# A two-layer gated attention kernel: K projection at steps 7 to 10, output projection at steps 13 to 16, and another order on GpSimd

## The chip, the cores and the metric

The kernel runs on one core of one Trainium2 chip. The metric is the device time of one execution in microseconds (us). A core has five engines with queues of their own, which meet only through semaphores: TensorE (PE, matmuls; its weight loads are shown as PEld), VectorE (DVE), ScalarE (ACT), GpSimd (POOL) and SyncE (SP, which here only issues DMAs).

## The reference, cut to what matters

x has 32 batches of 256 rows and 256 columns, each with a context of 120 rows and 512 columns. Four sublayers are added to x one after the other, each with a gate tanh(g):

```python
def xattn0(x, context, w_qkv, w_proj, b_proj):          # 16 heads of 16
    q, k, v = heads(x @ w_qkv.T)
    k = concat(heads_k(context), k); v = concat(heads_v(context), v)   # 120 + 256 keys
    attn = softmax(q * D ** -0.5 @ k.T)
    return (attn @ v) @ w_proj.T + b_proj
x = x + tanh(g_xattn[0]) * xattn0(layernorm(x), ctx, ...)
x = x + tanh(g_ffn[0])   * ternary_ffn(layernorm(x), ...)   # scale: max |x| over all batches
x = x + tanh(g_xattn[1]) * depool(layernorm(x), ctx, lens)  # recurrence over 120 patches
x = x + tanh(g_ffn[1])   * int8_ffn(layernorm(x), ...)
```

The second sublayer divides by one maximum over all batches. So the kernel has two phases: first the attention sublayer for all 32 batches, then a row phase with the other three. The change is in the first phase.

## The kernel before

**Loop and steps.** In the attention phase every engine runs the same loop over batches, `iterations`, each with its own `body` (a few batches are written out ahead of and behind a hardware loop over pairs). A body of batch b has 24 steps, u = 0 to 23. The engines don't share a clock for the steps; each works its list in order and waits on semaphores. A batch has 16 heads, 256 queries (two tiles of 128) and 376 keys in 3 tiles of 128.

**What TensorE does in a step.** `scores_t(u)`, line 592: two matmuls of transposed scores into one of three banks st_ps, of which ScalarE takes the exponential into probs (line 883, one for each step, at the end of the step on its list). Because of the three banks, the scores of step u wait for the exponential of step u - 3. `scores`, line 602: the same scores in the other layout (ms_ps, two banks), for batch b's last heads and the next batch's first 12 heads, of which VectorE takes the row maximum (line 787); one or two in a step, 32 in a batch. `attend`, line 617: 12 groups of matmuls of probs with V at steps 1, 7, 13 and 19, into pv_ps, which ScalarE copies out as oT (line 899).

**The jobs.** Between these stand the small products and transposes of the `JOBS` table. Two banks are shared, `misc` (0) and `aux` (1). An entry (bank, first step, steps, batch offset) says where a job's matmuls go; a job of four steps has one piece, two matmuls, in each. On misc: xT (transposes of the normalised rows), q, k and v (projections, lines 640 and 643) and proj (output projection, line 648). On aux: o0 to o3 (transposes of oT, line 664), aT (of the attention rows, line 669), neg0 and neg1 (of the split maxima, line 658) and kcT (of the context's keys, line 653). A job's first piece waits until the engine that reads the bank has taken the job before it (`s_free`), and the reader waits for `s_full`. ScalarE takes xT (line 904), q (918), k (951), kcT (945), v (962), aT (921) and the negs (891, followed by a DMA into q6, line 893); VectorE takes o0 to o3 (`normalise`, a reciprocal at line 794 and a multiplication at 796) and proj (line 829, which updates x).

**How Q and K come to the scores.** GpSimd splits qk, which holds Q, K and the context's keys of batch b + 2, into three bf16 parts: four instructions (lines 531 to 537) for each half m of the heads. SyncE's `stack` copies them with 12 DMAs for each half into q6 and k6, which the scores of step 6 (first half) and step 18 (second half) of the next body read. The maxima take a like way: GpSimd's `split_neg` (lines 468 to 474), neg0 or neg1 on TensorE, a copy and a DMA by ScalarE, and then the scores of step 0 or 12.

**GpSimd's order in a body:** maxima of the second half (b), the context's norm (485 to 493), the norm of x for b + 3 (498 to 504), a wait for ScalarE's normalised rows and the bias (507), distances (511), row statistics of b - 1 (515 to 518), maxima of the first half (b + 1), and both halves of the split (b + 2).

## Time and profile before

| | us |
|---|---|
| median of 3 runs (lowest to highest) | 1210.75 (1209.83 to 1213.24) |
| profiled execution | 1212.96 |
| its span, first to last instruction | 1211.2 |
| TensorE busy in it | 1078.1 (89%) |
| VectorE | 921.0 (76%) |
| ScalarE | 818.8 (68%) |
| GpSimd | 700.3 (58%) |

The granted TensorE clock was 1.00 through the attention phase, 0.97 over the span. The attention phase fills about four fifths of the span, the row phase the rest. Busy shares are means; TensorE's ends are modelled, so starts are the surer numbers. In a time line a row is a start, a duration, engine, line, operation, output and inputs, how many instructions were merged, and in brackets the idle time before it with what ended it. A row of several merged instructions has the duration of all together.

### The profile page before, as it was taken

Reading aid. Unit: us, or ns where it says so; the run is one execution under the profiler, and the core shown is the slowest. Engines: PE = TensorE matmul, PEld = TensorE weight load, DVE = VectorE, ACT = ScalarE, POOL = GpSimd, SP = SyncE. Lnnn points to the kernel's source line nnn. Section 1 sums busy time; section 2 is a strip of 40 time slices with the busy share of each in tenths; the row PEclk is TensorE's granted clock in tenths of the full one; section 3 lists DMA queues with packets and bytes.
Section 4 is the critical chain, followed back from the end, with each engine's and each line's share of the span. In section 5 each row is a group of like instructions: output and inputs, shape, how many; then the busy total and the mean of one; then the engine's idle time right before and its main releaser. Section 6 shows DMA issues by size and latency. Waiting matters only on the chain.

```text
span 1211.2 us, 33412 instructions
## 1 busy us (share of the span) xinstructions
PE 1078.1 (89%) x8458; PEld 706.5 (58%) x8458; DVE 921.0 (76%) x2328; ACT 818.8 (68%) x1730; POOL 700.3 (58%) x1259
## 2 busy tenths in 40 slices
PE   4599899989999999999999999999999886988885
PEld 3355555656565665555566555656655445877774
DVE  3877777767777777777777777777777646999997
ACT  2157666766777777677677777777766566888874
POOL 4355555555555555555555555555554416777776
PEclk9699999999999999999999999999999997999997
DMA  4233333333333333333333333333333300222232
GB/s 125 78 92 96 96 96 94 94 94 94 98 100 100 100 99 99 103 101 99 100 99 100 97 104 101 97 94 95 87 87 87 83 12 31 68 84 93 85 92 86
DMA packets 158681, 110.18 MB, mean 91 GB/s; under 512 B 17155, under 2 KB 154789, under 8 KB 158629
## 3 DMA queue, kind: packets, MB, share of 16 engines
q1 hardware_dynamic: 156900, 108.78, 33.1%
q10 hardware_dynamic: 1728, 0.79, 0.2%
q8 instruction: 23, 0.38, 0.1%
q14 instruction: 30, 0.24, 0.1%
HBM read 30.30 MB, written 16.29 MB: 38 GB/s over the span
## 4 chain that ended last, share of the span: by engine, by line
PE 33%; DVE 17%; issue 15%; POOL 15%; DMA 9%; SPq 5%; POOLq 2%; DVEq 2%; ACT 1%; ACTq 0%
PE pv_ps L617 8%; PE ms_ps L602 6%; PE st_ps L592 6%; DMA q<-parts 6%; POOL qk L533 4%; PE misc L648 4%; DVE neg L787 4%; PE misc L640 3%; SPq L394 3%; POOL parts L531 2%; POOL parts L535 2%; SPq L392 2%; POOL parts L537 2%; DMA q<-negT 2%; DVE am L1171 2%
## 5 line engine op out<-in xcount | busy, mean ns | idle before, releaser
L787 DVE TENSOR_REDUCE neg<-ms_ps 128x1 f32<-128x376 f32 x1024 | 533.0, 545 | 221.2 <-PE ms_ps L602 212.7
L883 ACT ACTIVATE probs<-st_ps 128x512 f32<-128x512 f32 x768 | 440.2, 603 | 103.2 <-PE st_ps L592 102.6
L602 PE MATMUL ms_ps<-k,q 96*128 96x376 bf16 x1024 | 334.7, 328 | 33.8 <-DMA q<-parts 25.2
L592 PE MATMUL st_ps<-q,k 99*128 99x256 bf16 x1536 | 295.3, 274 | 10.2 <-DMA q<-negT 6.9
L592 PEld LDWEIGHTS st_ps<-q,k 99*128 99x128 bf16 x1536 | 131.8, 98 | 140.3 <-issue 43.3
L617 PE MATMUL pv_ps<-probs,v 128*32 128x256 f32 (+1 forms) x3072 | 195.4, 387 | 0.1
L602 PEld LDWEIGHTS ms_ps<-k,q 96*128 96x128 bf16 x1024 | 98.8, 97 | 104.5 <-DVE neg L787 66.7
L640 PE MATMUL misc<-xnT,wqkvT 128*128 128x256 f32 x512 | 158.1, 394 | 1.5 <-ACT xnT L904 1.5
L507 POOL TENSOR_TENSOR xs<-xs,bias_p 128x256 f32 (+1 forms) x64 | 45.2, 727 | 161.0 <-ACT xn L941 161.0
L617 PEld LDWEIGHTS pv_ps<-probs,v 128*32 128x32 f32 (+1 forms) x3072 | 87.5, 110 | 81.2 <-issue 24.3
L640 PEld LDWEIGHTS misc<-xnT,wqkvT 128*128 128x128 f32 x512 | 95.0, 200 | 5.9 <-ACT xnT L904 2.3
L899 ACT COPY oT<-pv_ps 128x256 f32<-128x256 f32 x128 | 47.2, 369 | 74.2 <-PE pv_ps L617 74.1
L537 POOL TENSOR_TENSOR parts<-qk,parts 128x632 bf16<-128x632 f32 x64 | 88.8, 1387 | 13.1 <-POOL parts L535 13.1
L533 POOL TENSOR_TENSOR qk<-qk,parts 128x632 f32<-128x632 f32 x64 | 88.7, 1385 | 11.7 <-POOL parts L531 11.7
L643 PE MATMUL misc<-wqkvT,xnT 128*128 128x256 f32 x256 | 77.0, 382 | 0.3 <-ACT qk L951 0.3
L648 PE MATMUL misc<-wprojT,attnT 128*128 128x256 f32 x256 | 75.8, 379 | 0.8 <-ACT attnT L921 0.8
L1099 PE MATMUL st_ps<-winT,probs 128*128 128x256 f32 x256 | 66.6, 382 | 0.7 <-ACT probs L1219 0.7
L1067 PE MATMUL ms_ps<-ident,probs 128*128 128x128 f32 x256 | 44.0, 300 | 22.1 <-DVE probs L1196 14.2
L511 POOL TENSOR_SCALAR plug<-plug,iota_n 120x256 f32<-120x256 f32 x32 | 37.0, 1155 | 36.0 <-DMA plug<-plugs 36.0
L891 ACT COPY negT<-aux 24x256 bf16<-24x256 bf16 x64 | 23.2, 362 | 48.7 <-PE aux L658 48.7
L531 POOL TENSOR_SCALAR parts<-qk 128x632 bf16<-128x632 f32 x64 | 46.1, 720 | 15.5 <-issue 13.4
L535 POOL TENSOR_SCALAR parts<-qk 128x632 bf16<-128x632 f32 x64 | 46.3, 723 | 12.5 <-POOL qk L533 12.5
(185 smaller groups left out, 1751.6 us busy)
## 6 DMA issues: line engine op xcount, KB each, us to landing
k<-parts SPq DMA_DIRECT2D x384, 94.0 KB, 2.8
q<-parts SPq DMA_DIRECT2D x384, 64.0 KB, 2.5
xs<-in_x SPq DMA_DIRECT2D x32, 256.0 KB, 2.8
out_dram<-xn SPq DMA_DIRECT2D x32, 256.0 KB, 2.2
cx<-in_ctx SPq DMA_DIRECT2D x32, 240.0 KB, 3.3
recurrence_input<-u_in SPq DMA_DIRECT2D x32, 120.0 KB, 2.3
plug<-plugs SPq DMA_DIRECT2D x32, 120.0 KB, 3.5
powers<-gath SPq DMA_DIRECT2D x32, 120.0 KB, 3.3
```

Source lines behind the costliest of these rows:

```text
L531: pool.tensor_scalar(parts[:, m, 0, :], f, 1.0, 0.0, ALU.mult, ALU.add).then_inc(s_split, 1)
L533: pool.tensor_tensor(f, f, parts[:, m, 0, :], ALU.subtract).then_inc(s_split, 1)
L535: pool.tensor_scalar(parts[:, m, 1, :], f, 1.0, 0.0, ALU.mult, ALU.add).then_inc(s_split, 1)
L537: pool.tensor_tensor(parts[:, m, 2, :], f, parts[:, m, 1, :], ALU.subtract).then_inc(s_split, 1)
L592: mm = pe.matmul(st_ps[u % SR][:, j * S:(j + 1) * S], k6[0:KM, r, h, k * P:(k + 1) * P], q6[0:KM, r, h, :], start=True, stop=True)
L602: pe.matmul(ms_ps[t][:, 0:KEYS], q6[0:KR, r, h % HU, t * P:(t + 1) * P], k6[0:KR, r, h % HU, 0:KEYS], start=True, stop=True).then_inc(s_ms, 1)
L617: mm = pe.matmul(pv_ps[VW * j:VW * (j + 1), 0:S], v[0:rows, pB, k, HG * g + j, :], probs[0:rows, (2 * w + j // 2) % PR, j % 2 * S:(j % 2 + ...
L640: mm = pe.matmul(misc[:, x0 * S:(x0 + 1) * S], wqkvT[:, x1, at:at + P], xnT[:, par, x1, :], start=(x1 == 0), stop=(x1 == KT - 1), skip_gro ...
L643: mm = pe.matmul(misc[:, x0 * C:(x0 + 1) * C], xnT[:, opp, x1, x0 * P:(x0 + 1) * P], wqkvT[:, x1, 2 * C:3 * C], start=(x1 == 0), stop=(x1 ...
L648: mm = pe.matmul(misc[:, x0 * C:(x0 + 1) * C], attnT[:, x1, x0 * P:(x0 + 1) * P], wprojT[:, x1, :], start=(x1 == 0), stop=(x1 == KT - 1), ...
L787: dve.tensor_reduce(neg[:, m, t, h % HU:h % HU + 1], ms_ps[t][:, 0:KEYS], AX.X, ALU.max, negate=True).then_inc(s_red, 1)
L883: act.activation(probs[:, u % PR, :], st_ps[u % SR][:, :], ACT.Exp).then_inc(s_exp, 1)
```

## The change

The K projection moves from steps 14 to 17 to steps 7 to 10, the output projection from 8 to 11 to 13 to 16, and the context keys' transposes from step 12 to step 2. ScalarE's copies follow: K at step 11 instead of 18, the context's preparation at 0 instead of 10, the context keys at 3 instead of 15, the attention rows at 7 instead of 6; its two normalised halves stand at 10 and 12 instead of both at 13; the powers' exponential moves from 11 to 15. VectorE updates x at step 17 instead of 13, takes the statistics at 19 and 21 instead of 15 and 18, the row maxima and minima of x at 7 and 13 (both a batch later) instead of 19 and 7, and the powers' update at 23 instead of 20. On GpSimd the first half of the split comes ahead of the bias, then the maxima, the distances, the second half, and the row statistics last. SyncE stacks the first half ahead of the powers' store. What is computed stays the same.

```diff
         JOBS = {
-            "xT": (0, 0, 1, 2), "q": (0, 2, 4, 2), "proj": (0, 8, 4, -1), "k": (0, 14, 4, 2), "v": (0, 19, 4, 1),
-            "o3": (1, 4, 1, -1), "aT": (1, 6, 1, -1), "neg1": (1, 8, 1, 0), "o0": (1, 10, 1, 0),
-            "kcT": (1, 12, 1, 2), "o1": (1, 16, 1, 0), "neg0": (1, 20, 1, 1), "o2": (1, 22, 1, 0),
+            "xT": (0, 0, 1, 2), "q": (0, 2, 4, 2), "k": (0, 7, 4, 2), "proj": (0, 13, 4, -1), "v": (0, 19, 4, 1),
+            "kcT": (1, 2, 1, 2), "o3": (1, 4, 1, -1), "aT": (1, 6, 1, -1), "neg1": (1, 8, 1, 0), "o0": (1, 10, 1, 0),
+            "o1": (1, 16, 1, 0), "neg0": (1, 20, 1, 1), "o2": (1, 22, 1, 0),
         }
...
+                if live(b + 2):
+                    stack(b + 2, par, 0)
                 if live(b - 1):
                     own_wait(sp, s_decay, b)
                     sp.dma_start(powers_dram[b - 1], gath[0:NP, opp, :]).then_inc(d_pow[opp], 16)
-                if live(b + 2):
-                    stack(b + 2, par, 0)
...
                     pool.tensor_tensor(rn0[:, 2, :], rn0[:, 1, :], mv0[:, :, 0], ALU.mult).then_inc(s_rn0, 1)
+                if live(b + 2):
+                    split(b, 0, i, par, opp)
+                if live(b + 3):
+                    B = b + 3
                     pool.wait_ge(s_xn, B * 2 + 2)
                     for t in range(T):
                         pool.tensor_tensor(xs[:, B, t, :], xs[:, B, t, :], bias_p[:, :], ALU.add).then_inc(s_xb, 1)
+                if live(b + 1):
+                    split_neg(b + 1, 0, b)
                 if live(b):
 
                     own_wait(pool, d_plug[par], i * 16 + 16)
                     pool.tensor_scalar(plug[0:NP, par, :], plug[0:NP, par, :], 0.0, iota_n[0:NP, :], ALU.add, ALU.add).then_inc(s_dist, 1)
+                if live(b + 2):
+                    split(b, 1, i, par, opp)
...
-                if live(b + 1):
-                    split_neg(b + 1, 0, b)
-                if live(b + 2):
-                    for m in range(2):
-
...
-                    if u == 13 and live(b - 1):
+                    if u == 17 and live(b - 1):
...
-                    if u == 15 and live(b - 1):
+                    if u == 19 and live(b - 1):
...
-                    if u == 18 and live(b - 1):
+                    if u == 21 and live(b - 1):
...
-                    if u == 19 and live(b - 1):
+                    if u == 7 and live(b - 2):
+                        dve.tensor_reduce(mx1[:, bass.ds((b - 2) * T, T)], xs[:, b - 2, :, :], AX.X, ALU.max).then_inc(s_x1, 1)
+                    if u == 13 and live(b - 2):
+                        dve.tensor_reduce(mn1[:, bass.ds((b - 2) * T, T)], xs[:, b - 2, :, :], AX.X, ALU.min).then_inc(s_x1, 1)
+                    if isinstance(b, int) and b == LAST and u == 22:
                         dve.tensor_reduce(mx1[:, bass.ds((b - 1) * T, T)], xs[:, b - 1, :, :], AX.X, ALU.max).then_inc(s_x1, 1)
-                    if u == 7 and live(b - 2):
-                        dve.tensor_reduce(mn1[:, bass.ds((b - 2) * T, T)], xs[:, b - 2, :, :], AX.X, ALU.min).then_inc(s_x1, 1)
-                    if isinstance(b, int) and b == LAST and u == 21:
                         dve.tensor_reduce(mn1[:, bass.ds((b - 1) * T, T)], xs[:, b - 1, :, :], AX.X, ALU.min).then_inc(s_x1, 1)
-                    if u == 20 and live(b):
+                    if u == 23 and live(b):
...
                 for u in range(HS):
+                    if u == 0 and live(b + 2):
+                        act.wait_ge(d_cx[par], (i + 1) * 16 + 16)
+                        if live(b + 1):
+                            wait_full(act, b - 1, "kcT")
+                        for m in range(2):
...
+                        ins.then_inc(s_cxp, 1)
...
+                    if u == 3 and live(b + 2):
+                        wait_full(act, b, "kcT")
+                        if live(b + 1):
+                            act.wait_ge(s_split, (b + 2) * 8)
+                        act.copy(qk[:, :, 2 * S:FC], aux[:, 0:2 * P].rearrange("p (m r) -> p m r", m=2)[:, :, 0:NP]).then_inc(s_free[1], 1)
...
-                        if live(b + 1):
-                            act.wait_ge(s_split, (b + 2) * 8)
                         act.mul(qk[:, :, 0:S], misc[:, :].rearrange("p (m r) -> p m r", m=2), SCALE).then_inc(s_free[0], 1)
-                    if u == 6 and live(b - 1):
+                    if u == 7 and live(b - 1):
...
-                    if u == 10 and live(b + 2):
...
-                    if u == 13 and live(b + 3):
+                    if u == 10 and live(b + 3):
...
-                        for t in range(T):
-                            act.activation(xn[:, opp, t, :], xs[:, B, t, :], ACT.Identity, bias=rn0[:, 3, t:t + 1],
-                                           scale=rn0[:, 1, t:t + 1]).then_inc(s_xn, 1)
-                    if u == 15 and live(b + 2):
-                        wait_full(act, b, "kcT")
-                        act.copy(qk[:, :, 2 * S:FC], aux[:, 0:2 * P].rearrange("p (m r) -> p m r", m=2)[:, :, 0:NP]).then_inc(s_free[1], 1)
-                    if u == 11 and live(b - 1):
+                    if u in (10, 12) and live(b + 3):
+                        t = (u - 10) // 2
+                        act.activation(xn[:, opp, t, :], xs[:, b + 3, t, :], ACT.Identity, bias=rn0[:, 3, t:t + 1],
+                                       scale=rn0[:, 1, t:t + 1]).then_inc(s_xn, 1)
+                    if u == 11 and live(b + 2):
+                        wait_full(act, b, "k")
+                        act.copy(qk[:, :, S:2 * S], misc[:, :].rearrange("p (m r) -> p m r", m=2)).then_inc(s_free[0], 1)
+                    if u == 15 and live(b - 1):
                         act.wait_ge(s_plug, b)
                         act.activation(gath[0:NP, opp, :], gath[0:NP, opp, :], ACT.Exp, scale=-DT).then_inc(s_decay, 1)
-                    if u == 18 and live(b + 2):
-                        wait_full(act, b, "k")
-                        act.copy(qk[:, :, S:2 * S], misc[:, :].rearrange("p (m r) -> p m r", m=2)).then_inc(s_free[0], 1)
...
-                    if u == 19 and live(b + 1):
+                    if u == 17 and live(b + 1):
...
+                    if u == 21 and live(b + 1):
+                        neg_rows(b + 1, opp, 0, live(b))
```

GpSimd's new function `split(b, m, ...)` holds the same waits and the same four instructions as the loop that is taken out, for one half m.

Three places in the order, in the body of batch 1, which stands written out ahead of the hardware loop. First TensorE from step 11 to the first output of step 14; before, with the last piece of the output projection (line 648) in step 11, the context transposes (653) in step 12, the attention product (617) in step 13 and the K projection (640) in step 14:

```order
L592 MATMUL st_ps<-q,k 128x256 x2
L602 MATMUL ms_ps<-k,q 128x376
L648 MATMUL misc<-wprojT,attnT 128x256
L592 MATMUL st_ps<-q,k 128x256 x2
L602 MATMUL ms_ps<-k,q 128x376
L653 MATMUL aux<-ident,cxp 128x120 x2
L592 MATMUL st_ps<-q,k 128x256 x2
L602 MATMUL ms_ps<-k,q 128x376
L617 MATMUL pv_ps<-probs,v 32x256 x12
L592 MATMUL st_ps<-q,k 128x256 x2
L602 MATMUL ms_ps<-k,q 128x376
L640 MATMUL misc<-xnT,wqkvT 128x256
```

After, where the scores are lines 597 and 607 and the output projection is line 653:

```order
L597 MATMUL st_ps<-q,k 128x256 x2
L607 MATMUL ms_ps<-k,q 128x376
L597 MATMUL st_ps<-q,k 128x256 x2
L607 MATMUL ms_ps<-k,q 128x376
L597 MATMUL st_ps<-q,k 128x256 x2
L607 MATMUL ms_ps<-k,q 128x376
L653 MATMUL misc<-wprojT,attnT 128x256
L622 MATMUL pv_ps<-probs,v 32x256 x12
L597 MATMUL st_ps<-q,k 128x256 x2
L607 MATMUL ms_ps<-k,q 128x376
L653 MATMUL misc<-wprojT,attnT 128x256
```

Steps 11 and 12 hold nothing but scores now, and a piece of the output projection stands in front of the attention product of step 13.

ScalarE from the copy of the maxima (step 8) to the exponentials of steps 11 and 12; before:

```order
L891 COPY negT<-aux 24x256
L893 DMA q<-negT 3x8x256
L883 ACTIVATE probs<-st_ps 128x512 x2
L929 COPY cxp<-cx 120x128 x2
L883 ACTIVATE probs<-st_ps 128x512
L948 ACTIVATE gath<-gath 120x256
L883 ACTIVATE probs<-st_ps 128x512 x2
L936 ACTIVATE rn<-rn 128x2
L941 ACTIVATE xn<-xs,rn 128x256 x2
L883 ACTIVATE probs<-st_ps 128x512
```

After, where 889 is the exponential, 945 and 951 the normalisation, 955 the copy of K:

```order
L897 COPY negT<-aux 24x256
L899 DMA q<-negT 3x8x256
L889 ACTIVATE probs<-st_ps 128x512 x2
L945 ACTIVATE rn<-rn 128x2
L951 ACTIVATE xn<-xs,rn 128x256
L889 ACTIVATE probs<-st_ps 128x512
L955 COPY qk<-misc 128x2x256
L889 ACTIVATE probs<-st_ps 128x512
L951 ACTIVATE xn<-xs,rn 128x256
L889 ACTIVATE probs<-st_ps 128x512 x2
```

The first normalised half now stands ahead of the exponential of step 10, in the place of the context copy, and the copy of K follows that exponential.

VectorE from the row maxima of steps 13 to 15 to those of step 19; before, with the update of x (829) at step 13 and its statistics (834) at step 15:

```order
L787 TENSOR_REDUCE neg<-ms_ps 128x1 x4
L829 SCALAR_TENSOR_TENSOR xs<-misc,tg,xs 128x512
L787 TENSOR_REDUCE neg<-ms_ps 128x1 x3
L834 BN_STATS bn<-xs 128x6 x2
L787 TENSOR_REDUCE neg<-ms_ps 128x1
L794 RECIPROCAL rcp<-aux 128x8
L796 TENSOR_TENSOR attn<-aux,rcp 128x2x64
L787 TENSOR_REDUCE neg<-ms_ps 128x1 x3
L840 BN_AGGR mvt<-bn 128x2 x2
```

After, where 792 are the maxima, 834 the update of x, 839 its statistics:

```order
L799 RECIPROCAL rcp<-aux 128x8
L801 TENSOR_TENSOR attn<-aux,rcp 128x2x64
L792 TENSOR_REDUCE neg<-ms_ps 128x1 x2
L834 SCALAR_TENSOR_TENSOR xs<-misc,tg,xs 128x512
L792 TENSOR_REDUCE neg<-ms_ps 128x1 x2
L839 BN_STATS bn<-xs 128x6 x2
L792 TENSOR_REDUCE neg<-ms_ps 128x1 x3
```

Between the normalisation of step 16 and the V projection of step 19 there is now the update of x, with two maxima ahead of it.

## Rows read from the trace of the kernel before

**Rows 1.** Page, part 1: busy time, share of the span and instructions of each engine.

```profile
PE 1078.1 (89%) x8458; PEld 706.5 (58%) x8458; DVE 921.0 (76%) x2328; ACT 818.8 (68%) x1730; POOL 700.3 (58%) x1259
```

**Rows 2.** Chain that ended last, 400 to 560 us: start us, us, what.

```profile
445.79 0.73 POOL parts L531
...
456.36 0.33 PE ms_ps L602
...
485.27 0.33 PE ms_ps L602
```

**Rows 3.** Time line of TensorE, steps 6 and 8: columns as told above.

```profile
456.36 0.33 PE L602 MATMUL ms_ps<-k,q 96*128 96x376 bf16 x1 [0.75 <-DMA q<-parts]
456.58 0.63 PE L669 MATMUL aux<-ident,attn 128*128 128x128 f32 x4
...
459.88 0.28 PE L658 MATMUL aux<-identb,negp 128*24 128x128 bf16 x2
```

**Rows 4.** Time line of VectorE, step 5, the normalisation.

```profile
455.54 0.20 DVE L794 RECIPROCAL rcp<-aux 128x8 f32<-128x8 f32 x1
455.77 0.29 DVE L796 TENSOR_TENSOR attn<-aux,rcp 128x128 f32<-128x128 f32 x1
```

**Rows 5.** Time line of ScalarE, steps 8 to 18.

```profile
461.60 1.09 ACT L883 ACTIVATE probs<-st_ps 128x512 f32<-128x512 f32 x2 [1.04 <-PE st_ps L592]
462.57 0.71 ACT L929 COPY cxp<-cx 120x128 f32<-120x128 f32 x2
463.18 0.61 ACT L883 ACTIVATE probs<-st_ps 128x512 f32<-128x512 f32 x1
...
464.93 0.23 ACT L936 ACTIVATE rn<-rn 128x2 f32<-128x2 f32 x1
465.29 1.09 ACT L941 ACTIVATE xn<-xs,rn 128x256 f32 x2
...
469.92 0.59 ACT L951 COPY qk<-misc 128x512 f32<-128x512 f32 x1
```

**Rows 6.** Time line of TensorE, steps 12 to 20.

```profile
463.55 0.40 PE L653 MATMUL aux<-ident,cxp 120*128 120x120 f32 x2
463.84 0.39 PE L592 MATMUL st_ps<-q,k 99*128 99x256 bf16 x2
...
464.33 1.50 PE L617 MATMUL pv_ps<-probs,v 128*32 128x256 f32 x24
465.76 0.39 PE L592 MATMUL st_ps<-q,k 99*128 99x256 bf16 x2
...
468.38 0.38 PE L664 MATMUL aux<-ident,oT 128*128 128x128 f32 x2
...
470.64 0.62 PE L643 MATMUL misc<-wqkvT,xnT 128*128 128x256 f32 x2
...
472.63 0.39 PE L592 MATMUL st_ps<-q,k 99*128 99x256 bf16 x2
...
474.24 0.28 PE L658 MATMUL aux<-identb,negp 128*24 128x128 bf16 x2 [0.62 <-POOL negp L474]
```

**Rows 7.** Time line of VectorE, steps 13 to 18.

```profile
464.90 0.74 DVE L829 SCALAR_TENSOR_TENSOR xs<-misc,tg,xs 128x512 f32 x1
...
469.21 0.29 DVE L796 TENSOR_TENSOR attn<-aux,rcp 128x128 f32<-128x128 f32 x1
469.42 1.52 DVE L787 TENSOR_REDUCE neg<-ms_ps 128x1 f32<-128x376 f32 x3
```

**Rows 8.** Time line of GpSimd, the split's second half (first half: rows 2).

```profile
450.53 0.72 POOL L531 TENSOR_SCALAR parts<-qk 128x632 bf16<-128x632 f32 x1
```

**Rows 9.** Line 852: ns min/median/max, first and last start; then the first batch's time line.

```profile
L852 DVE SCALAR_TENSOR_TENSOR gath<-plug x32: 415/415/1181, 92.5 to 987.9; 120x256 f32<-120x256 f32 x32
...
92.07 1.38 POOL L533 TENSOR_TENSOR qk<-qk,parts 128x632 f32<-128x632 f32 x1 [0.18 <-POOL parts L531]
92.55 1.18 DVE L852 SCALAR_TENSOR_TENSOR gath<-plug 120x256 f32<-120x256 f32 x1
```

40 lines of the change are left out of this document (17 added, 23 removed).

## The prediction, made before the changed kernel ran

> **What bounds the kernel now.** I read the page's first part, then the chain of work that ended last, then the time lines of TensorE, ScalarE, VectorE and GpSimd for one batch, and compare starts with starts. TensorE is busy 89% of the span, VectorE 76% and ScalarE 68% [rows 1]. The profiled execution took 1212.96 us, the median of the runs is 1210.75; I add to the median. In the chain the same matmul returns after 485.27 - 456.36 = 28.91 us [rows 2]: that is one batch, and what lengthens or shortens it counts for each batch. The chain closes through GpSimd: the split of Q and K begins at 445.79, and the score matmul that reads its result starts at 456.36.
>
> At two places of the batch TensorE visibly waits for that late GpSimd work. At step 6 the scores of the next batch start at 456.36 with 0.75 us of idle time before them, put down to the DMA of the parts [rows 3]. At step 20 the transposes of the maxima start at 474.24 after 0.62 us of waiting for GpSimd [rows 6]. There are smaller holes, and they are what the change leans on: the scores of step 13 start at 463.84, and the exponential of step 10 began at 463.18 and took 0.61, so it ended at 463.79 [rows 5, 6]. There are three score banks, so step 13 must wait for step 10's exponential: here ScalarE sets the pace, not TensorE.
>
> I place the new work in this one batch, on the clock of before, from step 6 to step 6.
>
> **Step 6 and 7: a gain that is spent at once.** Now the K copy comes at step 11 instead of 18, and the split of the first half stands right behind the norm on GpSimd. It can start near 464.8. From the start of a split to the score matmul it took 456.36 - 445.79 = 10.57 us [rows 2]; so it is done near 475.4, and step 6 of the next batch is at 484. The wait at step 6 goes. What is late next is the transposes of the attention rows behind it: they wait for VectorE's normalisation, which starts its multiplication at 455.77 and takes 0.29, so they start at 456.12 instead of 456.58 [rows 3, 4], a gain of 0.46. But a piece of the K projection now stands in step 7. What a piece in front of the attention product costs: step 19's piece starts at 470.64 and step 20 at 472.63, 1.99 us, and the product alone takes 465.76 - 464.33 = 1.43 [rows 6], so 0.56. That is 0.1 more than the gain; the product had a small hole in front of it in step 7 that this piece fills. I take the net as zero: the transposes of the maxima at step 8 stay at 459.88 [rows 3].
>
> **Steps 8 to 14: +0.79 us.** ScalarE copies the maxima, issues their DMA and starts exponentials 8 and 9 at 461.60 as before [rows 5]. At 462.57 it had the context copy (0.71) and then exponential 10. Now it has at step 10 the small multiplication and one normalised half: 465.29 - 464.93 = 0.36 and half of 1.09 less overlap, 0.50 [rows 5]. Exponential 10 starts at 462.57 + 0.86 = 463.43, 0.25 later than before, and ends at 464.04. Scores of step 13 start at 464.09. Behind it on ScalarE stands the K copy: it starts 0.49 after exponential 10 (two take 1.09, one 0.60 [rows 5]), at 463.92, takes 0.59 [rows 5], ends at 464.51. The output projection's first piece is in step 13, and needs the bank that this copy frees: 464.57. With the 0.56 and the product's 1.43, step 14 starts at 466.56, against 465.76 before: **+0.79** (rounding the sum). What the change takes out of steps 11 and 12 (a projection piece, and the two context transposes with 463.84 - 463.55 = 0.29 [rows 6]) gives nothing back, as TensorE waits for exponential 10 anyway. The bounds of this term: 0.25 if only exponential 10 moved, 0.8 as worked out, and 1.0 if the DMA of the maxima is also late for step 12.
>
> **Steps 14 to 20: +0.38 us.** From step 14 to the transposes at step 16 it was 468.38 - 465.76 = 2.62 us [rows 6], with the same pieces in it, so these start at 469.17. The V projection at step 19 takes the bank that VectorE's update of x frees, and the update has moved from step 13, where 3 steps lay behind it, to step 17. VectorE must first do the normalisation (it needs the transposes, which last 0.38 [rows 6], so 469.17 + 0.42), one row maximum, a second, and then the update: 469.59 + 0.23 to the multiplication [455.77 - 455.54, rows 4], + 0.21 to the next maximum [469.42 - 469.21, rows 7], two maxima at a third of 1.52 each, and 0.74 for the update [rows 7]: 471.8. The V projection started at 470.64 [rows 6]; now at 471.81, **+1.17** in all, so +0.38 on top of 0.79. Queued on TensorE behind this waiting piece are the attention product of step 19 and all that follows. Low bound 0: VectorE could be earlier, as the statistics (step 15) left the stretch.
>
> **Step 20: -0.62 us.** With the maxima's split on GpSimd in front of the second half and of the row statistics, does TensorE still wait? Without a wait TensorE would come there 1.17 later and 0.62 earlier, at 474.24 + 1.17 - 0.62 = 474.79. On GpSimd the first half starts near 464.8 and takes 450.53 - 445.79 = 4.74 us [rows 2, 8], to 469.5. Two bias additions and four small instructions lie between that and 474.79, and the last maximum that the four need ends on VectorE at about 471.1 (469.59 + 0.23 + 0.21 + 0.5 + 0.55). That leaves 3.7 us for four instructions on 16 columns. The wait of 0.62 [rows 6] goes whole: +1.17 - 0.62 = +0.55. What it would cost if GpSimd were late after all: up to that 0.62 again.
>
> **Step 2: +0.29 us.** The context transposes now stand in step 2, where TensorE has no hole, at 0.29 us [rows 6]. The context copy on ScalarE at step 0 (0.71) has cover: its next reader, the first Q piece at step 2, is 2 us on, behind the attention product.
>
> **Sum.** 0.79 + 0.38 - 0.62 + 0.29 = 0.84 us a batch; each start is read to about 0.05, and I round down to 0.8. Batches with all of it are 28 of 32: the first has no output projection, the last three lack the normalisation or K. 28 x 0.8 = 22.4, and 1210.75 + 22.4 = **1233 us**. Prologue, tail and the row phase after the attention keep their work: 0, within 2 us. The extra moves cost nothing where cover is long: SyncE's powers store behind the first half's 12 DMAs, the second half of the split (its reader is step 18 of the next batch), the two reductions over x at steps 7 and 13 instead of 19 and 7.
>
> [...] VectorE's update of the recurrence powers reads the same SBUF tile twice. Its median is 0.415 us and its longest 1.181 [rows 9]: at 92.55 it began while GpSimd's subtraction of the split (92.07, 1.38 long) ran, and took 1.18. The change moves it to step 23, beside the second half's split, at nearly each batch. On VectorE this is 0.77 us more, and the next maxima are late by that. TensorE then needs them at step 2, behind the 1.43 us product of step 1, so I count 0. [...]
>
> **Rivals.**
> Rival 1, faster: both new waits are covered. TensorE is late for step 13 by no more than now, because ScalarE reaches exponential 10 earlier once TensorE no longer stalls at step 6, and the update of x finds VectorE empty since the statistics have left steps 15 to 18. For it: VectorE is busy only 76% [rows 1]. Against: starts at 463.79 and 463.84 fit too well for slack. Then only -0.62 + 0.29 remains, -0.33 a batch, and with the 0.1 or so that step 7 may keep, -0.4: 28 x 0.4 = 11, **1199.5 us**. It decides if the K copy ends before TensorE is at step 13.
> Rival 2, no change: the first term is 0.25 (the K copy is covered) and the second 0: 0.25 - 0.62 + 0.29 = -0.08, about **1209 us**.
> Rival 3, slower still: the 0.77 us of the blocked update is not covered at step 1. 28 x 0.77 = 21.6 more, 1255 us; with half of it covered **1244 us**. Against: the product of step 1 lies between.
> The change does what it says: steps and queue order are fixed in the program.
>
> **Chances.** Forecast (1224 to 1242 us): 0.62. Rival 1: 0.20. Rival 2: 0.10. Rival 3: 0.08. A measurement of this kernel tells a change from none at about 0.3%, 3.6 us. Slower by more: 0.62 + 0.08 = 0.70; within: 0.10; faster: 0.20. The range of 8 in 10 reaches to 1200, which takes in Rival 2 and the slower half of Rival 1, and to 1244 for Rival 3: 1200 to 1244.
>
> **What the profile of the changed kernel would show.** The chain's period would be 29.7 us instead of 28.91. No idle time for the DMA of the parts before the scores of step 6, and none for GpSimd before the transposes of step 20. The scores of step 13 would start about 4.2 us after the transposes of step 8 (now 463.84 - 459.88 = 3.96), and the output projection's first piece within 0.1 us of the K copy's end. The V projection would start within 0.1 us of the end of VectorE's update of x. The update of the powers would take about 1 us in most batches. I am wrong if the output projection's first piece follows its scores with no hole, or if the V projection waits for its maxima alone; and if ScalarE stands at step 0 for the context load, a further term is missing.

## The result and the profile after

The changed kernel took 1234.54 us, the median of 4 runs (1233.35 to 1236.48), beside 1211.99 us for the kernel before (4 runs, 1209.83 to 1214.72). The ratio is 1.0186 with a 95% interval of 1.0159 to 1.0213: slower. The prediction was 1233 us.

Part 1 of the page of the changed kernel, which answers to rows 1, and the shares of its chain by engine:

```profile
PE 1083.7 (88%) x8458; PEld 711.5 (58%) x8458; DVE 923.6 (75%) x2328; ACT 826.0 (67%) x1730; POOL 703.8 (57%) x1259
...
PE 54%; DVE 18%; issue 11%; ACT 5%; POOL 4%; DMA 4%; DVEq 1%; ACTq 1%; POOLq 0%; SPq 0%
```

The engines do the same work as before in a longer span. GpSimd has 4% of the chain that ended last, where it had 15% in the kernel before. The loop through its split, which the prediction followed in rows 2, is open: TensorE no longer waits for the parts. The other engines' waits now make up the period. The chain of the changed kernel in the same stretch, 400 to 560 us (start, us, what):

```profile
464.65 0.63 PE aux L674 x4
...
473.34 0.73 POOL parts L485
...
478.08 0.72 POOL xs L528
479.49 0.75 DVE xs L834
...
494.34 0.63 PE aux L674 x4
```

The GpSimd rows in it are no wait. The chain takes the last event of a semaphore for the releaser, and the update of x (L834) does wait for the semaphore of the bias additions (L528); but by the program it needs only the additions of its own batch, which were made three bodies earlier, and VectorE had no idle time before 479.49.

The period is 494.34 - 464.65 = 29.69 us. In the kernel before it was 28.91 from one score matmul to the next [rows 2], and 28.95 from these transposes (456.58) to the next ones (485.53). TensorE's time line of one batch of the changed kernel, steps 6 to 20 (columns as in rows 3: start, us, engine, line, what, and in brackets the idle time before it and what ended it). L674 are the attention rows' transposes, L663 those of the maxima (steps 8 and 20), L597 the scores, L653 the output projection, L648 the V projection:

```profile
464.65 0.63 PE L674 MATMUL aux<-ident,attn 128*128 128x128 f32 x4 [0.43 <-DVE attn L801]
...
468.38 0.28 PE L663 MATMUL aux<-identb,negp 128*24 128x128 bf16 x2
...
472.29 0.39 PE L597 MATMUL st_ps<-q,k 99*128 99x256 bf16 x2 [0.97 <-DMA q<-negT]
...
472.68 0.38 PE L597 MATMUL st_ps<-q,k 99*128 99x256 bf16 x2
472.90 0.32 PE L607 MATMUL ms_ps<-k,q 96*128 96x376 bf16 x1
473.06 0.65 PE L653 MATMUL misc<-wprojT,attnT 128*128 128x256 f32 x2
473.65 1.50 PE L622 MATMUL pv_ps<-probs,v 128*32 128x256 f32 x24
475.09 0.39 PE L597 MATMUL st_ps<-q,k 99*128 99x256 bf16 x2
...
480.28 0.70 PE L648 MATMUL misc<-wqkvT,xnT 128*128 128x256 f32 x2 [0.32 <-DVE xs L834]
...
483.27 0.28 PE L663 MATMUL aux<-identb,negp 128*24 128x128 bf16 x2
```

From these starts and those of rows 3 and 6 the batch can be cut at the same five places in both kernels. The last column is the mean difference over the batches whose attention transposes start between 270 and 870 us (21 before, 20 after). All numbers in us:

| stretch | before | after | difference | the prediction's term | mean difference |
|---|---|---|---|---|---|
| attention transposes, step 6, to maxima transposes, step 8 | 3.30 | 3.73 | +0.43 | +0.46 (gain of step 6 given back) | +0.44 |
| to the scores of step 14 | 5.88 | 6.71 | +0.83 | +0.79 | +0.96 |
| to the V projection, step 19 | 4.88 | 5.19 | +0.31 | +0.38 | +0.31 |
| to the maxima transposes, step 20 | 3.60 | 2.99 | -0.61 | -0.62 | -0.63 |
| to the attention transposes of the next batch | 11.29 | 11.07 | -0.22 | -0.46 + 0.29 | -0.20 |
| period | 28.95 | 29.69 | +0.74 | +0.84 | +0.88 |

The batch shown is one of the shorter ones (they last 29.45 to 30.05). What varies is the second stretch, from 6.54 to 7.06.

The spans of the two profiled executions differ by 1231.6 - 1211.2 = 20.4 us. Of these, 3.3 are there before the first attention transposes (103.6 and 106.9 us). The six batches behind them give back 0.7, since the kernel before had slow batches there (up to 30.81). The next 20 batches cost 17.6, and the rest 0.2.

The waits that the prediction named on other engines are there too. ScalarE, then VectorE, of the same batch:

```profile
469.17 0.75 ACTq L899 DMA_DIRECT2D q<-negT  x1
...
471.92 0.58 ACT L889 ACTIVATE probs<-st_ps 128x512 f32<-128x512 f32 x1
472.39 0.57 ACT L955 COPY qk<-misc 128x512 f32<-128x512 f32 x1
```

```profile
479.49 0.74 DVE L834 SCALAR_TENSOR_TENSOR xs<-misc,tg,xs 128x512 f32 x1
```

The update of x ends at 480.23 and the V projection starts at 480.28, and TensorE waited for it. The copy of K ends at 472.96 and the first piece of the output projection starts at 473.06, but this piece did not wait: it follows the scores before it (472.90) after 0.16 us, as it does in the kernel before. So it is in 16 of the 20 batches; in the other four it comes after 0.24, which is 0.05 behind the end of the copy. That the piece would follow with no hole was one of the prediction's own signs of being wrong.

What held TensorE there was not in the sum. At step 12 (472.29) it waits 0.97 us for the small DMA that brings the negated maxima into q, and that DMA was issued at 469.17, 3.12 us earlier; in the middle batches this wait is 0.46 to 1.39 us. In the kernel before, the scores of step 12 start 2.42 us after the issue in nearly all batches, without a wait. So two things stand behind each other at steps 12 to 14, this DMA and ScalarE's order, and end at nearly the same time. The first experiments take them apart.

### The profile page after: what moved, and what is told of

Same layout as the page of the kernel before. It is cut to its first block, busy times and chain, and to the rows that moved or that the text cites. A ratio compares the mean times of both kernels' runs of the same rounds, so it can differ in the third digit from the quotient of the medians.

```text
span 1231.6 us, 33435 instructions
## 1 busy us (share of the span) xinstructions
PE 1083.7 (88%) x8458; PEld 711.5 (58%) x8458; DVE 923.6 (75%) x2328; ACT 826.0 (67%) x1730; POOL 703.8 (57%) x1259
## 4 chain that ended last, share of the span: by engine, by line
PE 54%; DVE 18%; issue 11%; ACT 5%; POOL 4%; DMA 4%; DVEq 1%; ACTq 1%; POOLq 0%; SPq 0%
PE pv_ps L622 14%; PE st_ps L597 9%; PE ms_ps L607 8%; PE misc L645 7%; PE misc L648 5%; DMA q<-negT 3%; PE misc L653 3%; DVE neg L792 3%; ACT probs L889 2%; DVE xs L834 2%; PE aux L674 2%; DVE am L1178 2%; DVE xs L1167 2%; PE misc L637 1%; PE aux L669 1%
## 5 line engine op out<-in xcount | busy, mean ns | idle before, releaser
L889 ACT ACTIVATE probs<-st_ps 128x512 f32<-128x512 f32 x768 | 445.4, 602 | 100.2 <-PE st_ps L597 99.4
L597 PE MATMUL st_ps<-q,k 99*128 99x256 bf16 x1536 | 294.9, 273 | 35.4 <-ACT probs L889 16.5
L597 PEld LDWEIGHTS st_ps<-q,k 99*128 99x128 bf16 x1536 | 131.6, 98 | 163.5 <-ACT probs L889 63.9
L468 POOL TENSOR_SCALAR negp<-neg 128x16 bf16<-128x16 f32 x64 | 13.1, 205 | 201.9 <-DVE neg L792 201.8
L491 POOL TENSOR_TENSOR parts<-qk,parts 128x632 bf16<-128x632 f32 x64 | 88.8, 1387 | 12.4 <-POOL parts L489 12.4
L648 PE MATMUL misc<-wqkvT,xnT 128*128 128x256 f32 x256 | 81.0, 398 | 9.7 <-DVE xs L834 9.7
L653 PE MATMUL misc<-wprojT,attnT 128*128 128x256 f32 x256 | 77.3, 385 | 0.8 <-ACT attnT L938 0.8
L648 PEld LDWEIGHTS misc<-wqkvT,xnT 128*128 128x128 f32 x256 | 44.6, 194 | 18.7 <-DVE xs L834 16.9
L1106 PEld LDWEIGHTS st_ps<-winT,probs 128*128 128x128 f32 x256 | 46.4, 191 | 7.7 <-ACT probs L1226 2.1
```

What stands on the lines that cost most here:

```text
L491: pool.tensor_tensor(parts[:, m, 2, :], f, parts[:, m, 1, :], ALU.subtract).then_inc(s_split, 1)
L597: mm = pe.matmul(st_ps[u % SR][:, j * S:(j + 1) * S], k6[0:KM, r, h, k * P:(k + 1) * P], q6[0:KM, r, h, :], start=True, stop=True)
L648: mm = pe.matmul(misc[:, x0 * C:(x0 + 1) * C], xnT[:, opp, x1, x0 * P:(x0 + 1) * P], wqkvT[:, x1, 2 * C:3 * C], start=(x1 == 0), stop=(x1 ...
L653: mm = pe.matmul(misc[:, x0 * C:(x0 + 1) * C], attnT[:, x1, x0 * P:(x0 + 1) * P], wprojT[:, x1, :], start=(x1 == 0), stop=(x1 == KT - 1), ...
L889: act.activation(probs[:, u % PR, :], st_ps[u % SR][:, :], ACT.Exp).then_inc(s_exp, 1)
L1106: pe.matmul(m1_ps[q][:, t * C:(t + 1) * C], yxT[:, k, t * P:(t + 1) * P], winT[:, k, :], start=(k == 0), stop=False)
```

## Experiments

Each ratio is that of the kernel to the kernel before, with its 95% interval.

**Steps 12 to 14: two holds.** `e2_xn12` takes ScalarE's first normalised half out from ahead of exponential 10, so that the K copy comes earlier.

```diff
-if u in (10, 12) and live(b + 3):
-    t = (u - 10) // 2
+if u == 12 and live(b + 3):
+    for t in range(T):
```

> The changed kernel with both normalised halves at step 12 on ScalarE, none at step 10, so that exponential 10 and the K copy come 0.5 us (one half) sooner. Theory A (step 13 waits for ScalarE's exponential 10, the projection for the K copy): steps 13 and 14 come 0.3 to 0.5 us sooner, 8 to 14 us less than the changed kernel, 1221 to 1226 us. Rival D (the DMA of the maxima lands 3.0 to 3.5 us after its issue and holds step 12, with step 13 0.4 behind it): no gain, 1232 to 1236 us.

Measured: 1232.93 us, ratio 1.0162 [1.0145, 1.0179], as rival D had it. `e3_sp` leaves ScalarE alone. On SyncE the plug load (the distances' input) goes ahead of the store of the recurrence input, and this store goes behind the first stacks and the powers' store.

```diff
-sp.dma_start(input_dram[b + 1], u_in[0:NP, opp, :]).then_inc(d_dep[opp], 16)
...
 sp.dma_start(plug[0:NP, par, :], plug_dram[b].partition_broadcast(NP)).then_inc(d_plug[par], 16)
...
 stack(b + 2, par, 0)
...
 sp.dma_start(powers_dram[b - 1], gath[0:NP, opp, :]).then_inc(d_pow[opp], 16)
+sp.dma_start(input_dram[b + 1], u_in[0:NP, opp, :]).then_inc(d_dep[opp], 16)
```

> The changed kernel with the SyncE order of the run e4 alone: distances' load ahead, recurrence input's store behind the first half's stack and the powers' store. Rival D expects the step 12 landing at 2.4 us instead of 3.3 behind its issue; since exponential 10 ends 4.16 us behind the transposes of step 8 and the K copy 4.6, the gain is only what the landing adds on top, 0.1 to 0.3 us a batch: 1226 to 1232 us. Theory A expects no change.

Measured: 1233.47 us, 1.0176 [1.0147, 1.0205]: no change, as theory A had it. But the landing did come earlier, as rival D had it. `e4_xn12_sp` has both edits.

> As the one before, and on SyncE the store of the recurrence input stands behind the first half's stack and the powers' store, and the distances' load goes out earlier, so that neither goes out beside the DMA of the maxima for step 12. If the landing at step 12 is late because of these two (rival D), it falls from 3.3 us behind its issue to about 2.4, and together with the earlier exponential 10 steps 13 and 14 come 0.8 us sooner: 1208 to 1214 us. If only ScalarE counts (theory A), this is the same as the one before.

Measured: 1222.47 us, 1.0079 [1.0058, 1.01]. Each edit alone gives next to nothing, both together 12 us, though less than was expected (1208 to 1214). The lines of TensorE at step 12 and 13, first of e2_xn12, then of e3_sp:

```profile
470.28 0.39 PE L597 MATMUL st_ps<-q,k 99*128 99x256 bf16 x2 [0.90 <-DMA q<-negT]
```

```profile
469.89 0.39 PE L597 MATMUL st_ps<-q,k 99*128 99x256 bf16 x2
...
470.99 0.39 PE L597 MATMUL st_ps<-q,k 99*128 99x256 bf16 x2 [0.35 <-ACT probs L889]
471.21 0.33 PE L607 MATMUL ms_ps<-k,q 96*128 96x376 bf16 x1
471.46 0.70 PE L653 MATMUL misc<-wprojT,attnT 128*128 128x256 f32 x2
```

In e2_xn12 the DMA wait is left: its maxima DMA was issued at 467.22, 3.06 us before. In e3_sp step 12 (469.89) comes 2.28 us after the issue (467.61), and now step 13 waits for exponential 10, as the prediction had reckoned it, and the output projection's piece starts 0.05 us behind the end of the K copy (in all 20 middle batches). From the maxima transposes to step 14's scores one batch takes 6.71 us in the changed kernel, 6.58 in e2_xn12 (466.43 to 473.01), 6.71 in e3_sp (466.82 to 473.53), 6.26 in e4_xn12_sp (460.65 to 466.91), and 5.88 before. The means over the middle batches are 6.84, 6.72, 6.73, 6.27 and 5.88. So the prediction's cause, ScalarE's order, is by itself enough for +0.85 (e3_sp), and the late DMA, with the K copy still early enough not to be waited for, for +0.84 (e2_xn12). The changed kernel, which has both, has +0.96. With both gone +0.39 is left: in e4_xn12_sp the K copy (464.21, 0.58 long) still ends only just ahead of the piece (464.84) that takes its bank.

**Steps 17 to 20: the update of x.** `e1_v20` moves the V projection one step later.

```diff
-"v": (0, 19, 4, 1),
+"v": (0, 20, 4, 1),
```

> The changed kernel with the V projection at steps 20 to 23 instead of 19 to 22. Theory: the V projection waits 0.6 us at step 19 for VectorE's update of x, with the attention product queued behind it. One step later it does not wait, and the product of step 19 starts about 1 us sooner; the last piece, in step 23, then makes the transposes of step 0 wait about 0.5 us for the V copy. Net about -0.5 us a batch: 1215 to 1223 us. If the update of x is not what holds step 19, the V piece only moves: no change against the changed kernel, or slower by the wait at step 0.

Measured: 1219.55 us, 1.007 [1.0045, 1.0094], as expected. The V projection's wait for VectorE (0.32 us before 480.28 above) is gone from all batches, and with it 15 us. In the middle batches the stretch from the scores of step 14 to the maxima's transposes of step 20 is 1.01 us shorter (7.16 instead of 8.17), and the one behind it, to the attention transposes, 0.46 longer, near the 1 and 0.5 of the expectation; the period is 0.53 shorter. That is more than the wait of 0.32. The move also puts one V piece behind the transposes of step 20, and how much of the gain comes from that was not taken apart.

`e9_three` joins the three edits.

> The changed kernel with three single changes together: both normalised halves at step 12, SyncE's order of the run e3, the V projection at steps 20 to 23. Alone, the first two together gave -0.0107 of the time of before and the third -0.0116. If the two new waits (step 12 to 13, and step 19) are separate terms of a sum, they add: ratio 0.995 to 0.999 to before, 1206 to 1211 us. If both are faces of one loop, the sum falls short: 1.002 to 1.007.

Measured: 1211.72 us, 0.9983 [0.9965, 1.0002]. The ratio lies in the range of a sum (0.995 to 0.999), and one loop (1.002 or more) is ruled out. With the edits against three holds the moved kernel is as fast as the kernel before. The sum is not quite reached, and the trace shows why: the spans of the profiled executions fell by 14.8 us (e1_v20) and 12.0 (e4_xn12_sp), but by 21.7 together, because the DMA of the maxima is now late at step 0. One batch:

```profile
388.28 0.39 PE L597 MATMUL st_ps<-q,k 99*128 99x256 bf16 x2 [1.05 <-DMA q<-negT]
```

This DMA was issued at 384.64, 3.64 us earlier. Beside it SyncE issued the store of the recurrence input (384.34) and the context load (385.04). In four of 21 batches it was on time, used 2.42 us after its issue without a wait; these batches last 28.75 us, less than the 28.93 of the kernel before, and the others from 28.89 to 29.47.

**Step 2: the context transposes.** `e8_kct12` puts them back at step 12, and ScalarE's copy of their result at step 13.

```diff
-"kcT": (1, 2, 1, 2),
+"kcT": (1, 12, 1, 2),
```

> The changed kernel with the context keys' transposes back at step 12 and ScalarE's copy of them at step 13 (the check that the split before is done then stands at step 6 again); the context copy stays at step 0. Theory: at step 2 the two transposes cost TensorE 0.2 to 0.3 us a batch, at step 12 nothing, as TensorE waits there anyway; 6 to 8 us less than the changed kernel, 1226 to 1229 us. The rival, that the hole at step 12 and 13 is not there to be used (the copy on ScalarE delays what follows), expects no change or up to 6 us more.

Measured: 1255.29 us, 1.0337 [1.0302, 1.0371]: 21 us slower than the changed kernel, outside of both theories. Step 2 did lose its transposes, but at step 12 they cost about the same: they stand behind the scores of step 12, and TensorE's wait is ahead of these. The stretch from step 8 to step 14 is 0.20 us longer in the mean. And step 0 now waits, for the same kind of DMA as step 12. TensorE of e8_kct12 at step 0, then ScalarE's issue, then SyncE's issues around it:

```profile
526.17 0.39 PE L597 MATMUL st_ps<-q,k 99*128 99x256 bf16 x2 [1.44 <-DMA q<-negT]
```

```profile
522.58 0.75 ACTq L899 DMA_DIRECT2D q<-negT  x1
```

```profile
522.12 0.37 SPq L416 DMA_DIRECT2D powers<-gath  x1
522.84 0.35 SPq L420 DMA_DIRECT2D cx<-in_ctx  x1
```

The maxima DMA is used 3.59 us after its issue. SyncE issued the context load (240 KB) 0.26 us behind it. In the changed kernel the same two went out at 482.06 and 482.76, ahead of the maxima DMA at 484.06, and step 0 used it at 486.33, 2.27 us after its issue:

```profile
482.06 0.37 SPq L416 DMA_DIRECT2D powers<-gath  x1
482.76 0.35 SPq L420 DMA_DIRECT2D cx<-in_ctx  x1
```

The reason for the shift is the split. It now needs ScalarE's copy of the context keys at step 13, and starts 10.57 us after the attention transposes instead of 8.69; SyncE's stacks and what is queued behind them come later with it (the context load 20.00 after the transposes instead of 18.11).

The batches of e8_kct12 itself tell what the wait costs. In three of 20 the DMA was on time (used after 2.29 to 2.31 us), and they last 29.55, 29.59 and 29.69 us; the 17 others last 30.42 to 30.97. A rival is VectorE's update of the powers, which is longer here in many batches, where it runs beside GpSimd's L491 (median of all 1.36 us instead of 0.454). It is not the cause: three of the 17 have it at 0.41 to 0.42, and last 30.80, 30.88 and 30.91.

`e11_kct12_late` is e8_kct12 with these two taken away from there: they become a function `small`, which the second stacks call behind their first part, and the context copy goes from step 0 to step 3.

```diff
+if part == 0 and mid is not None:
+    mid()
...
-stack(b + 2, par, 1)
+stack(b + 2, par, 1, small)
...
-if u == 0 and live(b + 2):
+if u == 3 and live(b + 2):
```

> e8_kct12 with SyncE's powers' store and context load put behind the first piece of the second stacks, and ScalarE's context copy moved from step 0 to step 3 to go with them. In e8_kct12 these two went out at 0.46 us ahead of and 0.26 us behind the small maxima DMA, which then landed 3.3 us after its issue, and TensorE waited for it at step 0 (1.44 us in one batch). Theory D (what SyncE issues beside the maxima DMA makes it late): with both gone from there it lands after 2.3 us again, about 1.0 us a batch less: 1226 to 1233, ratio 1.012 to 1.018. Rival (the lateness is that of ScalarE's own queue, or of the stacks that are issued at all times): no change against e8_kct12, 1251 to 1257, ratio 1.032 to 1.037.

Measured: 1352.32 us, 1.1169 [1.1131, 1.1206]. Neither time. The edit cost far more elsewhere, since the context load came after the copy that reads it: on the page that copy shows 121.7 us of idle time ahead of it, behind which all of ScalarE's queue stood.

```profile
L919 ACT COPY cxp<-cx 120x128 f32<-120x128 f32 x64 | 22.7, 403 | 121.7 <-DMA cx<-in_ctx 121.7
```

So its time says nothing of the question. The wait itself does: the scores of step 0 started 2.27 to 2.30 us after the issue of the maxima DMA in each of 19 batches in the middle of the run, where e8_kct12 has a mean of 3.27 in 20 batches. With the store and the load gone from beside it the DMA was on time in each batch. That fits SyncE's issues as the cause; as e11_kct12_late has a period of 33.7 us and much else moved with it, this run alone would not show it.

**GpSimd's order, done alone.** The change also puts the split of the maxima ahead of the row statistics. Could the kernel before have that without the rest? `e5_neg_first` does it.

```diff
+if live(b + 1):
+    split_neg(b + 1, 0, b)
 if live(b - 1):
     own_wait(pool, s_x1, (b - 1) * 6 + 4)
...
-if live(b + 1):
-    split_neg(b + 1, 0, b)
```

> The kernel before with one swap on GpSimd: the maxima's split of the next batch ahead of the row statistics; nothing else moves. My theory is that the kernel before was held by one loop through GpSimd: statistics of VectorE, GpSimd's statistics, its four maxima instructions, both halves of the split, the DMAs of the parts, the scores of step 6. The swap leaves the sum on GpSimd as it is, so it frees the transposes of step 20 (their 0.62 us of waiting goes) but the split ends no sooner: the wait at step 6 grows by the same amount and the period stays 28.9 us. Expected ratio to before 0.995 to 1.002, 1205 to 1213 us. The rival, that each of the two waits costs its own time, expects 0.62 x 30 = 19 us less, 1192 us.

Measured: 1191.8 us, 0.9834 [0.9818, 0.985]. The expectation of no change fell and the rival was right: it had put 0.62 us a batch on the wait at step 20. GpSimd of the kernel before at step 19 and 20, then of e5_neg_first:

```profile
500.30 0.19 POOL L515 COPY mv<-mvt 128x4 f32 x1 [1.18 <-DVE mvt L840]
...
501.72 0.20 POOL L468 TENSOR_SCALAR negp<-neg 128x16 bf16<-128x16 f32 x1
...
503.64 0.72 POOL L531 TENSOR_SCALAR parts<-qk 128x632 bf16<-128x632 f32 x1 [0.50 <-issue]
```

```profile
513.50 0.20 POOL L468 TENSOR_SCALAR negp<-neg 128x16 bf16<-128x16 f32 x1 [1.09 <-DVE neg L787]
...
514.98 0.19 POOL L517 COPY mv<-mvt 128x4 f32 x1
...
516.42 0.98 POOL L531 TENSOR_SCALAR parts<-qk 128x632 bf16<-128x632 f32 x1
```

TensorE of e5_neg_first at step 6:

```profile
527.32 0.33 PE L602 MATMUL ms_ps<-k,q 96*128 96x376 bf16 x1 [0.77 <-DMA q<-parts]
```

Before, GpSimd stood still for the statistics' result of VectorE (mvt), with the maxima's split and the Q and K split queued behind. Now the four small instructions fill that wait, and the Q and K split starts 516.42 - 513.50 = 2.92 us after the first of the seven small instructions instead of 503.64 - 500.30 = 3.34, and that first one no longer waits for mvt. It waits for the row maxima instead (1.09 us), and starts 14.19 us after the attention transposes where it was 14.77. The Q and K split thus starts 17.11 us after these transposes (499.31) instead of 18.11 (485.53). Its first instruction loses 0.26 of that again (0.98 instead of 0.72, below). The wait for the parts at step 6 stays at 0.77 us: the loop is still closed through GpSimd, and shorter; from the score matmul at 499.08 to that at 527.32 it is 28.24 us instead of 28.91.

`e6_stat_last` puts the statistics last, behind both halves of the split.

> The kernel before with its row statistics last on GpSimd, behind the maxima's split and both halves of the split; no projection moves and no copy moves. This is the gaining half of the change alone. Theory: the split starts about 1.8 us sooner, the waits of steps 20 and 6 both go, and the transposes of the attention rows are then held by VectorE's normalisation (0.46 gained there). -0.62 and -0.46 a batch, 30 batches: about 32 us less, 1175 to 1185 us. The rival, that ScalarE and VectorE hold the kernel at nearly the same period without GpSimd, expects less than 10 us of gain.

Measured: 1201.49 us, 0.9914 [0.9895, 0.9932]: a gain of 12 us instead of about 32, and less than that of e5_neg_first. VectorE's update of the powers (L851 here) had been moved, in time, onto GpSimd's subtraction. The line's durations in ns (min/median/max), then one batch of GpSimd, VectorE and TensorE:

```profile
L851 DVE SCALAR_TENSOR_TENSOR gath<-plug x32: 415/1578/1590, 90.0 to 971.9; 120x256 f32<-120x256 f32 x32
```

```profile
521.34 1.38 POOL L526 TENSOR_TENSOR qk<-qk,parts 128x632 f32<-128x632 f32 x1 [0.18 <-POOL parts L524]
```

```profile
521.42 1.58 DVE L851 SCALAR_TENSOR_TENSOR gath<-plug 120x256 f32<-120x256 f32 x1
```

```profile
523.52 0.33 PE L601 MATMUL ms_ps<-k,q 96*128 96x376 bf16 x1 [0.65 <-DVE neg L786]
```

The update began 0.08 us behind GpSimd's instruction and ended (523.00) 0.28 behind its end (522.72): 1.58 us instead of 0.415. TensorE waited for the row maxima behind it. `e7_gath19` moves that update from step 20 to step 19.

```diff
-if u == 20 and live(b):
+if u == 19 and live(b):
```

> The run e6 with one thing more: VectorE's update of the powers (two inputs in SBUF) at step 19 instead of 20. In e6 it takes a median of 1.58 us instead of 0.42, since it begins just behind GpSimd's subtraction of the split (1.38 us), and TensorE then waits 0.65 us for a row maximum at step 23. One step sooner GpSimd still has the four small instructions. If the blocked instruction is what ate the gain of e6, it takes 0.42 us again, the wait at step 23 goes and the period falls by 0.7 to 0.8 us: 1174 to 1182 us. If something else holds step 23 (the DMA of the maxima for step 0, or ScalarE), the run stays at 1197 to 1203 us.

Measured: 1192.75 us, 0.9833 [0.9804, 0.9862]. The update is short again, and the wait for the maxima at step 23 is gone:

```profile
L851 DVE SCALAR_TENSOR_TENSOR gath<-plug x32: 414/436/443, 89.0 to 962.8; 120x256 f32<-120x256 f32 x32
```

So the longer update beside GpSimd's instruction cost 9 us (1201.49 to 1192.75). But 1174 to 1182 was expected. TensorE now waits for the maxima DMA, at step 12 and at step 0:

```profile
507.39 0.39 PE L591 MATMUL st_ps<-q,k 99*128 99x256 bf16 x2 [0.45 <-DMA q<-negT]
...
521.18 0.39 PE L591 MATMUL st_ps<-q,k 99*128 99x256 bf16 x2 [0.56 <-DMA q<-negT]
```

`e10_neg_g19` is e5_neg_first with the same earlier update, since in e5_neg_first GpSimd's L531 (the first instruction of the split; the expectation calls it the distance instruction) took 0.98 us beside it instead of 0.72.

> The kernel before with GpSimd's maxima split ahead of the row statistics (as in e5_neg_first) and the gather of the powers' update one step earlier (step 19, as in e7_gath19). Theory lock: in e5_neg_first GpSimd's distance instruction took 0.98 us instead of 0.72 since VectorE's two-input update began beside it; 0.26 of GpSimd's chain comes back, but step 6 waits for the input's DMA as before, so between 0 and 0.26 us a batch times 28: 1184.5 to 1192, ratio 0.977 to 0.983. Theory no change (a DMA holds the rest): 1190 to 1194, ratio 0.982 to 0.985.

Measured: 1190.23 us, 0.9818 [0.9796, 0.984]. L531 has a maximum of 0.724 us again, but the period is the same within 0.03 us, and the interval overlaps that of e5_neg_first: the "no change" of the two theories, though the time alone would fit either. It has the lowest time of all that ran, and e5_neg_first, with one block moved, has nearly all of the gain.

## Why the prediction was right

The sum came out, and each of its terms is near what was measured. But at the largest term the wait that held TensorE was another than the one it was reckoned from, and in the step from the batch to the kernel some luck helped. Point by point, in the prediction's own steps:

- **Step 6 and 7, net zero.** Right. The wait for the parts is gone, the attention transposes wait for VectorE's normalisation (0.43 us, L801), and the K piece at step 7 gives back what step 6 gained: +0.43 against +0.46.
- **Steps 8 to 14, +0.79.** The size is near (+0.83 in the batch shown, +0.96 in the mean), and e3_sp shows that ScalarE's order alone makes +0.85. But in the changed kernel it is the late DMA of the maxima that holds TensorE, in each batch, and the output projection waits for the K copy in only four of 20. The prediction had this DMA as an upper bound of 1.0, with no row behind it; that bound is what happened. The two causes lie over each other, so the sum held; that the DMA alone makes nearly the same +0.84 (e2_xn12) is a coincidence. Whoever had cured the one that the prediction names would have gained 1.6 us by the medians, which is within the noise.
- **Steps 14 to 20, +0.38.** Right: +0.31, with the V projection 0.05 us behind the end of VectorE's update. e1_v20 shows that this wait counts.
- **Step 20, -0.62.** Right: GpSimd's wait is gone, -0.61.
- **Step 2, +0.29.** The term was a little too large. In the changed kernel the transposes take 0.21 us from their start to the next instruction:

```profile
490.17 0.37 PE L658 MATMUL aux<-ident,cxp 120*128 120x120 f32 x2
490.38 0.32 PE L607 MATMUL ms_ps<-k,q 96*128 96x376 bf16 x1
```

  ScalarE did not stand at step 0 for the context load: its context copy starts at 486.90 with no idle time before it. The reading that this is a plain cost which could be had back did not hold: e8_kct12 paid it at step 12 instead, and the wait that then came up at step 0 made the kernel 21 us slower.
- **28 batches of 0.8, and 0 for the rest.** Lucky in part. The full batches cost 0.88 and not 0.8, but there are about 20 of them; the first six cost nothing, and 3.3 us came up ahead of the first attention transposes, where the prediction had put 0, within 2. What these 3.3 are was not taken apart.
- **The update of the powers, about 1 us in most batches.** Wrong in size. Its median in the changed kernel is 0.454 us:

```profile
L858 DVE SCALAR_TENSOR_TENSOR gath<-plug x32: 415/454/1650, 99.6 to 1010.5; 120x256 f32<-120x256 f32 x32
```

  At 487.06 in the batch above it started just as GpSimd's last split instruction (485.85, 1.39 long) was ending at 487.24. The place of the update, step 23, was read from the order; the time at which GpSimd would be in its instruction was not worked out to the tenth, and that decides. That the update is delayed beside GpSimd's split is what the other runs show too: it was in most batches of e6_stat_last (median 1.578 us against 0.415 in the kernel before), and in none of e7_gath19 (0.436). Where it was delayed it ended 0.28 us behind the end of GpSimd's instruction: at 93.73 behind 93.45 in the kernel before [rows 9], at 523.00 behind 522.72 in e6_stat_last. The other way round, with VectorE's update begun just ahead, GpSimd's L531 took 0.98 us against 0.72, in e5_neg_first. What in the hardware makes the two delay each other was not shown.
- **Rival 1, faster** (0.20) would have needed slack in steps 12 to 20. The VectorE share of 76% did not give any: the V projection's wait showed up within 0.1 us of where it was put, and so did the K copy's once the DMA was cured (e3_sp). **Rival 3** was not put to the test in the changed kernel, since one update in 32 was over 1 us there (1.65). In e1_v20 29 of 32 are (median 1.47 us), and the kernel was 15 us faster all the same.

What the prediction did not say is that its gaining term could be had alone. It put -0.62 us a batch on the wait at step 20, against +1.46 for the rest of the change. e5_neg_first shows that a like reordering in the kernel before, four small instructions ahead of the statistics, is worth 0.67 us a batch (28.91 to 28.24), and 1.7% of the time. All else in the change, the moved projections and copies with what they bring along, then costs 43 us against that (1234.54 to 1191.8).

## What to carry to other kernels

Where an engine waits, look for a second wait that ends at nearly the same time: a cure of one shows nothing, and only the pair of edits, alone and together, tells. A time that comes out as predicted does not show the cause; look in the trace for the hole that was predicted. Of several moves in one change, price each alone: here the reordering of four small instructions ahead of a block that waits was worth 1.7%, and the rest of the change took back more than that. A move on one engine can be paid on a DMA half a batch away, so look there too: with the context transposes and their copy moved to steps 12 and 13, the 12 KB DMA of step 0 was used 3.59 us after its issue in e8_kct12, with another queue's 240 KB load issued 0.26 us behind it, and 2.27 us in the changed kernel, with that load 1.30 us ahead.

## What the runs showed of the hardware

- The 12 KB DMA of the maxima, issued by ScalarE, was used 2.2 to 2.3 us after its issue in all middle batches at step 12 of e3_sp and e9_three and step 0 of e11_kct12_late, where none of the loads and stores of 120 to 256 KB went out within 1 us of it and TensorE was ready for it. With such issues beside it, it was mostly used after 3.0 to 3.8 us (step 12 of the changed kernel and e2_xn12, step 0 of e8_kct12 and e9_three). The use differed with the distance: with the context load of 240 KB issued 1.30 us ahead of the maxima DMA it came after 2.27 us (changed kernel), with the load 0.62 ahead (e3_sp: 481.87 and 482.49) after 2.50, with the load 0.26 behind (e8_kct12) after 3.59. But distance alone does not decide it. In e9_three the load goes out 0.4 us behind the DMA in each of the 20 batches up to 840 us; 16 times the DMA is used after 3.2 to 3.8 us, and four times after 2.42. By which of the loads or stores, and through what, it is held, was not taken apart. Nor was e7_gath19's 2.4 to 3.2 us, where the stacks stand beside it.
- VectorE's update of the powers, 0.415 us in the kernel before (median), took 1.58 us in e6_stat_last where it began 0.08 us behind a GpSimd instruction of 1.38 us (521.42 and 521.34), and ended 0.28 us behind it. GpSimd's instruction kept its time (1.38; L533, the same one, has a median of 1.385 in the kernel before). The other way round, GpSimd's L531 of 0.72 us took 0.98 where VectorE's instruction had begun just before it (both are listed at 516.42 in e5_neg_first).
